# Two-layer cross-attention kernel on one core: queries' x loaded with features on partitions and normalised there, row statistics sent through DRAM; unit 0's row sums moved ahead

## The reference

```python
h = layernorm(x)                          # per row: (x - mean) / sqrt(var + 1e-5)
q = rope(h @ Wq)                          # 32 heads of 128
k = rope(ctx @ Wk); v = ctx @ Wv          # 8 heads of 128
logits = 30 * tanh(q @ k.T / sqrt(128) / 30)
w = softmax(where(mask, logits, -1e30))
x = x + (w @ v) @ Wo
```

## Time and profile before

| | |
|---|---|
| median of 3 runs | 824.38 us (824.3 to 824.47) |
| the profiled execution, its own time | 825.46 us |
| its span | 823.7 us |
| PE busy | 815.2 us (99%) |
| DVE, POOL, ACT busy | 591.5, 430.0, 403.7 us |
| mean granted TensorE clock | 0.996 |

### The profile page before, as it was taken

One profiled execution on the slowest core, in us unless ns is written; L12 is line 12 of the kernel. 1 busy time (PEld: TensorE's weight loads), 2 busy tenths in 40 slices (PEclk: granted clock), 3 DMA queues, 4 the chain that ended last, 5 costly groups with the idle time before them and its releaser, 6 DMA issues.

```text
span 823.7 us, 12087 instructions
## 1 busy us (share of the span) xinstructions
PE 815.2 (99%) x4310; PEld 674.5 (82%) x4310; DVE 591.5 (72%) x1133; ACT 403.7 (49%) x980; POOL 430.0 (52%) x341
## 2 busy tenths in 40 slices
PE   9999999899999999999999999999999999999998
PEld 7898877677777778777778788898988888888887
DVE  6874449889797988879788656464365667677894
ACT  6542114332334332343431532667797877777762
POOL 4665449874769667677864620113232531366442
PEclk9999999899999999999999999999999999999999
DMA  8545310413233223322311840002011200300002
GB/s 313 228 152 170 91 61 4 128 53 104 77 103 102 78 65 88 118 64 77 103 53 54 296 119 14 26 27 52 14 39 26 65 27 14 128 14 2 0 1 103
DMA packets 33244, 67.00 MB, mean 81 GB/s; under 512 B 5152, under 2 KB 8480, under 8 KB 32544
## 3 DMA queue, kind: packets, MB, share of 16 engines
q1 hardware_dynamic: 30640, 61.38, 24.0%
q10 hardware_dynamic: 2544, 4.85, 1.6%
HBM read 54.55 MB, written 11.67 MB: 80 GB/s over the span
## 4 chain that ended last, share of the span: by engine, by line
PE 73%; POOL 1%; issue 1%; DVE 0%; ACT 0%; DMA 0%; ACTq 0%; POOLq 0%
PE PB L1814 14%; PE PB L1816 13%; PE PB L1815 13%; PE PB L1862 11%; PE PB L2077 8%; PE PB L2092 3%; PE PB L1821 3%; PE PB L2004 3%; PE PB L1987 2%; PE PB L2025 1%; PE PB L2039 0%; POOL W L1200 0%; DMA stage<-in_wo 0%; POOL WVl L1200 0%; POOL WSl L1200 0%
## 5 line engine op out<-in xcount | busy, mean ns | idle before, releaser
L1237 POOL TENSOR_TENSOR qb<-qb,arena 128x512 f32<-128x512 f32 x76 | 99.6, 1316 | 126.2 <-DVE arena L1656 126.2
L1314 ACT ACTIVATE Oh<-PB 96x128 fp32r<-96x128 f32 (+2 forms) x236 | 79.3, 359 | 45.7 <-PE PB L2004 26.6
L1528 DVE TENSOR_TENSOR xs<-xs,PB 128x512 f32<-128x512 f32 x111 | 73.2, 682 | 36.8 <-PE PB L1816 27.9
L1200 POOL TENSOR_TENSOR WVl<-stage,WVh 128x512 fp32r<-128x512 f32 (+1 forms) x25 | 31.6, 1278 | 70.6 <-ACT WVh L1314 64.0
L1653 DVE TENSOR_TENSOR qb<-PB,ropeq 128x512 f32<-128x512 f32 x64 | 44.0, 688 | 26.6 <-PE PB L1816 16.1
L1814 PE MATMUL PB<-WVh,Oh 128*128 128x512 f32 x158 | 62.3, 394 | 0.8 <-DVE arena L1656 0.4
L1815 PE MATMUL PB<-WVl,Oh 128*128 128x512 f32 x158 | 61.5, 390 | 0.0
L1816 PE MATMUL PB<-WVh,Ol 128*128 128x512 f32 x158 | 61.5, 389 | 0.0
L1314 ACT ACTIVATE WSh<-wsum 128x1024 fp32r<-128x1024 f32 x12 | 12.7, 1061 | 90.8 <-POOL wsum L1182 90.8
L1814 PE MATMUL PB<-W,Oh 128*128 128x512 f32 x142 | 55.5, 391 | 0.6 <-POOL W L1200 0.6
L1815 PE MATMUL PB<-W,Oh 128*128 128x512 f32 x142 | 55.3, 389 | 0.0
(11 more groups left out here) (336 smaller groups left out, 2464.4 us busy)
## 6 DMA issues: line engine op xcount, KB each, us to landing
stage<-in_wq SPq DMA_DIRECT2D x44, 256.0 KB, 2.8
stage<-in_wo SPq DMA_DIRECT2D x44, 256.0 KB, 2.8
arena<-recs SPq DMA_DIRECT2D x32, 256.0 KB, 3.9
stage<-in_wk SPq DMA_DIRECT2D x12, 256.0 KB, 4.4
keys<-qb SPq DMA_DIRECT2D x12, 256.0 KB, 2.3
arena<-keys SPq DMA_DIRECT2D x6, 512.0 KB, 3.3
xs<-in_x SPq DMA_DIRECT2D x8, 256.0 KB, 6.6
ctx_hi<-cTh SPq DMA_DIRECT2D x1, 2048.0 KB, 7.4
```

The source lines that it names most:

```text
L1200: e.tensor_tensor(lo, src, hi.bitcast(f32), ALU.subtract).then_inc(s_wlo)
L1237: e.tensor_tensor(dst, dst, tmp, ALU.add).then_inc(s_radd)
L1314: return e.activation(dst, src, ACT.Copy)
L1528: e.tensor_tensor(xs[:, i, :], xs[:, i, :], PB[b][:, :], ALU.add).then_inc(free[b])
```

## The change

x is loaded a second time, transposed on the host (`xT`, 2 MB, four DMAs), into xf. DVE packs the reciprocal deviations and the negative mean times deviation of four tiles (two copies of 128x4), turns them with one transpose, and SyncE sends them as rows to DRAM (4 DMAs of 8 partitions) and reads them back broadcast to all partitions (2 DMAs), once for each half of the rows. DVE then normalises xf in place: for each half and each pair of feature chunks a multiplication and an addition of 128x1024 (`x_norm`, 8 instructions in all). ACT takes the high part and DVE the low part (`x_split`, 4 of 128x1024 on each). The 32 transposes on PE, the 8 `xn`, the 16 copies on ACT and the 8 `xsplit` on DVE go. In the plan the second four `stats` and `rstd` move ahead of three ropes, `v0(0, 3)` moves ahead of `k0(0, 1)`, `xt` moves behind `k0(5, 0)`, `ctx_out` (the store of the split ctx, 4 MB) moves there too, and the banks are dealt anew. In unit 0 `sum0` and its DMAs move ahead of `xt_split` and of two ropes; in unit 1 `norm0(0)` moves ahead of `q0p(1, 2)`, and `q0p(1, 2)` and `q0p(1, 3)` take banks 2 and 3.

```diff
     for i in LO:
         step("stats", 0, i)
     step("rstd", 0, 0)
+    step("xT_load")
+    step("stat_out", 0)
+    step("stat_in", 0)
...
-    for i in range(2):
-        stage("xT", 0, i)
-    ring[:] = [0, 1, 4, 6, 5, 2, 7]
+    ring[:] = [4, 5, 1, 6, 7, 0, 2]
+    stage("v0", 0, 3)
     stage("k0", 0, 1)
     step("rope", "k0", 1, 0)
...
+    for i in HI:
+        step("stats", 0, i)
+    step("rstd", 0, 4)
+    step("stat_out", 1)
+    step("stat_in", 1)
     step("rope", "k0", 0, 1)
+    k0(1, 1)
+    split("wk0", 3)
+    v0(0, 4)
+    k0(2, 0)
     stage("many")
     split("wv0", 1, 0)
     split("wv0", 1, 1)
...
     v0(0, 5)
-    for i in (4, 5):
-        step("xn", 0, i)
+    step("x_norm", 0, 0)
     k0(2, 1)
     spill_k(2, 0)
     split("wk0", 4)
     v0(0, 6)
     spill_k(2, 1)
...
+    step("x_norm", 1, 0)
     k0(3, 0)
+    for kk in range(2):
+        step("x_split", kk, 0)
     v0(0, 7)
...
     k0(3, 1)
+    step("x_norm", 0, 1)
     split("wk0", 5)
     v0(1, 0)
     spill_k(3, 1)
-    step("xt")
     v0(1, 1)
     k0(4, 0)
+    step("x_norm", 1, 1)
     split("wvq", 0)
...
     k0(4, 1)
+    for kk in range(2):
+        step("x_split", kk, 1)
     split("wk0", 6)
...
     k0(5, 0)
+    step("xt")
     split("wq0", 0)
     v0(1, 6)
+    step("ctx_out")
...
             burst(0)
             q0p(0, 1, 7)
             q0(1, 2, bank=1)
-            for k in range(2):
-                for h in range(2):
-                    step("xt_split", k, h)
+            step("sum0", 0)
+            step("sum0_out", 0)
+            for hf in range(2):
+                step("xt_split", 0, hf)
+            step("xt_split", 1, 0)
             q0p(0, 2, 0)
             q0p(0, 3, 4)
-            step("sum0", 0)
-            step("sum0_out", 0)
+            step("xt_split", 1, 1)
...
             q0p(1, 1, 1)
-            q0p(1, 2, 0)
+            norm0(0)
+            q0p(1, 2, 2)
             step("pair", 2)
-            norm0(0)
-            q0p(1, 3, 4)
+            q0p(1, 3, 3)
...
+                elif kind == "stat_out":
+                    hf, = k
+                    sp.wait_ge(s_turned, hf + 1)
+                    for b in range(4):
+                        e.dma_start(stat[:, 512 * hf:512 * hf + 512].rearrange("m (i b t) -> b m i t", b=4, t=32)[b],
+                                    pair[32 * b:32 * b + 8, 32 * hf:32 * hf + 32]).then_inc(s_sout, 16)
+                elif kind == "stat_in":
+                    hf, = k
+                    cols = slice(512 * hf, 512 * hf + 512)
+                    sp.wait_ge(s_sout, 64 * (hf + 1))
+                    for m in range(2):
+                        e.dma_start(stat_at[m][:, cols], stat[m, cols].unsqueeze(0).broadcast_to([128, 512])).then_inc(s_sin0[hf], 16)
...
+                elif kind == "x_norm":
+                    kk, hf = k
+                    x = xf[:, 2 * kk:2 * kk + 2, 512 * hf:512 * hf + 512]
+                    by, plus = (t[:, 512 * hf:512 * hf + 512].unsqueeze(1).broadcast_to([128, 2, 512]) for t in stat_at)
+                    for c in (2 * kk, 2 * kk + 1):
+                        dve.wait_ge(s_ldt[c], 16)
+                    dve.wait_ge(s_sin0[hf], 32)
+                    e.tensor_tensor(x, x, by, ALU.mult).then_inc(s_xm)
+                    dve.wait_ge(s_xm, 2 * hf + kk + 1)
+                    e.tensor_tensor(x, x, plus, ALU.add).then_inc(s_xf)
+                elif kind == "x_split":
+                    kk, hf = k
+                    lo, src, hi = (H[:, 2 * kk:2 * kk + 2, 512 * hf:512 * hf + 512] for H in (xTl, xf, xTh))
+                    dve.wait_ge(s_xhi, 2 * hf + kk + 1)
+                    e.tensor_tensor(lo, src, hi.bitcast(f32), ALU.subtract).then_inc(s_xlo)
```

More of the change, by code:

```diff
@@ L3 @@
 from contextlib import ExitStack
-INS = ["x", "ctxT", "tab", "lowtri", "wq0", "wk0", "wv0", "wvq", "wo0", "aw", "bcat",
+INS = ["x", "xT", "ctxT", "tab", "lowtri", "wq0", "wk0", "wv0", "wvq", "wo0", "aw", "bcat",
        "wq1", "wk1", "wv1", "wo1", "w1", "a1", "bf1", "coef", "scl", "bias"]
@@ L240, in plan @@
     split("wv0", 1, 1)
-    for i in HI:
-        step("stats", 0, i)
-    step("rstd", 0, 4)
-    k0(1, 1)
-    v0(0, 4)
-    step("ctx_out")
-    split("wk0", 3)
-    k0(2, 0)
     v0(0, 5)
-    for i in (4, 5):
-        step("xn", 0, i)
+    step("x_norm", 0, 0)
     k0(2, 1)
@@ L256, in plan @@
     spill_k(2, 1)
-    for i in (4, 5):
-        stage("xT", 0, i)
-        step("xn", 0, i + 2)
-        step("xsplit", 0, i)
+    step("x_norm", 1, 0)
     k0(3, 0)
+    for kk in range(2):
+        step("x_split", kk, 0)
     v0(0, 7)
@@ L264, in plan @@
     spill_k(3, 0)
-    for i in (6, 7):
-        stage("xT", 0, i)
-        step("xsplit", 0, i)
     k0(3, 1)
+    step("x_norm", 0, 1)
     split("wk0", 5)
@@ L829, in program @@
         wk0_1 = qb[:, 1, 0:512]
+        stat_at = [Eb[:, :, :].rearrange("p h c -> p (h c)"), rsum]
         small = []
@@ L1091, in sync_program @@
                     e.dma_start(xs[:, i, :], a["x"][i * 128:(i + 1) * 128, :]).then_inc(s_ldx[i], 16)
+                elif kind == "xT_load":
+                    for c in range(4):
+                        e.dma_start(xf[:, c, :], a["xT"][c * 128:(c + 1) * 128, :]).then_inc(s_ldt[c], 16)
+                elif kind == "stat_out":
[10 more added lines that the diff above has]
+                        e.dma_start(stat_at[m][:, cols], stat[m, cols].unsqueeze(0).broadcast_to([128, 512])).then_inc(s_sin0[hf], 16)
                 elif kind == "sum0_out":
@@ L1381, in scalar_program @@
                     move(xTh[:, :, 128 * i:128 * i + 128], src).then_inc(s_xhi)
-                    if ph == 0:
-                        move(xf[:, :, 128 * i:128 * i + 128], src).then_inc(s_xf)
+                elif kind == "x_split":
+                    kk, hf = k
+                    src, hi = (H[:, 2 * kk:2 * kk + 2, 512 * hf:512 * hf + 512] for H in (xf, xTh))
+                    act.wait_ge(s_xf, 2 * hf + kk + 1)
+                    move(hi, src).then_inc(s_xhi)
                 elif kind == "v0_move":
@@ L1396, in scalar_program @@
                     elif i < 2:
-                        act.wait_ge(*done("xT", 0, 7))
+                        act.wait_ge(s_xm, 4)
                     else:
@@ L1600, in vector_program @@
                     e.tensor_tensor(to[:, :], PB[bank_of("p", u, t)][:, :], kept, ALU.add).then_inc(s_cmb)
+                elif kind == "stat_out":
+                    hf, = k
+                    r = slice(4 * hf, 4 * hf + 4)
+                    dve.wait_ge(s_one, 2)
+                    dve.wait_ge(s_ln, 10 * (hf + 1))
+                    e.tensor_copy(psum32[:, 0:4], lnb[:, 1, r]).then_inc(s_stat)
+                    e.tensor_copy(psum32[:, 4:8], lnb[:, 4, r]).then_inc(s_stat)
+                    dve.wait_ge(s_stat, 2 * hf + 2)
+                    e.transpose(pair[:, 32 * hf:32 * hf + 32], psum32[:, :]).then_inc(s_turned)
+                elif kind == "x_norm":
[8 more added lines that the diff above has]
+                    e.tensor_tensor(x, x, plus, ALU.add).then_inc(s_xf)
+                elif kind == "x_split":
+                    kk, hf = k
+                    lo, src, hi = (H[:, 2 * kk:2 * kk + 2, 512 * hf:512 * hf + 512] for H in (xTl, xf, xTh))
+                    dve.wait_ge(s_xhi, 2 * hf + kk + 1)
+                    e.tensor_tensor(lo, src, hi.bitcast(f32), ALU.subtract).then_inc(s_xlo)
                 elif kind == "xt":
                     b = {(kk, hf): xf[:, 2 * kk:2 * kk + 2, 512 * hf:512 * hf + 512] for kk in range(2) for hf in range(2)}
-                    dve.wait_ge(s_xf, 8)
+                    dve.wait_ge(s_xlo, 4)
                     e.tensor_tensor(b[1, 0], b[1, 0], b[0, 0], ALU.subtract).then_inc(s_xt)
@@ L1834, in tensor_program @@
                     pe.wait_ge(*lo_ready("wp", u, t // 2))
-                    pe.wait_ge(*read("xT", 0, 4 * hf + 3))
+                    pe.wait_ge(*x_ready(hf))
                     for c in range(4):
@@ L1845, in tensor_program @@
                     pe.wait_ge(*(lo_ready("wp", u, t // 4) if t in (1, 2, 4) else (s_wslo, u - PLAIN + 1)))
-                    for i in (3, 7):
-                        pe.wait_ge(*read("xT", 0, i))
+                    pe.wait_ge(*x_ready(1))
                     if t in (4, 5, 6, 7):
@@ L1928, in tensor_program @@
                         pe.wait_ge(s_whi, splits["wq0", 0] + 1)
-                        pe.wait_ge(*read("xT", 0, 3))
+                        pe.wait_ge(*x_ready(0))
                         for c in range(4):
```

34 lines of the change are left out of this document (16 added, 18 removed).

## The result

The change takes 828.10 us (median of 6, 826.86 to 828.36) where the kernel before takes 824.28 (median of 6, 823.97 to 824.47): ratio 1.0045, 95% interval [1.0034, 1.0056]. It is slower by 3.8 us, inside the range, and 2.9 above the forecast of 825.2. The profiled execution took 828.36 us, span 826.6. In two of the nine executions of `combo`, further down, the clock was granted at 0.557 and 0.249 and they took 1351 and 3160 us; its ratio leaves them out, and so does the median given there.

The account below looks back on a forecast made before the run. PE was taken as the bound, busy 815 of 823.7 us. Terms -3.9 + 4.85 - 0.1 = +0.85 gave 826.3 us for a profiled execution, 825.2 as a median; range 818.5 to 829.5.

Parts of the forecast that it names:

- rival (a): First stage: PE's idle time before k0(7,0) drops the clock to 1.2 GHz, costing 3.2 us, giving 828.4; chance 0.22.
- PE's own work, -3.9: First stage: 32 transposes leave PE, 3.46 us plus 0.4 for switching, all of it on the path.
- The chain of DVE: First stage: DVE's instructions priced in order, x_norm(0,0) beginning at 31.75 and the rope of k0(5,1) ending at 76.2.
- rival (d): First stage: statistics arrive late behind xT, x_norm(0,0) starts 3 to 4 us late; 828 to 829, chance 0.10.
- Sum of waits, +4.85 forecast: First stage: PE waits for POOL's low parts, about 1.8 us at k0(6,0), 0.2 at k0(4,0), 2.85 at k0(7,0).
- The burst, -0.1: Burst of unit 2: norm0(0)'s wait goes, but POOL's additions and wo0 splits hold PE instead; net -0.1 us.
- the frame: Whole sum made against the profiled execution of 825.46 us, 1.08 above the median of 824.38.

Follow-up runs that it names:

- combo: The change with xt between k0(7,0) and k0(7,1), wk0 6 and 7 splits ahead of ropes, and unit 0's ropes ahead of DVE's two xt_split; 821.87 us, ratio 0.9970.
- before_burst: The kernel before with the change's orders and banks of units 0 and 1, unit 0's ropes ahead of DVE's xt_split, high parts first in e0(0,0); 823.87 us.
- ctx_out_back: The change with ctx_out, the store of 4 MB, back in its old place behind v0(0,4); 828.35 us, ratio 1.0049.
- low_last: The change with k0 from j = 2 on and v0(1,0) taking products with the weight's high part first, low part last; 825.83 us, ratio 1.0011.
- burst_only: The kernel before with only the change's new order and banks of units 0 and 1; 824.96 us, ratio 1.0000.
- filled: The change with ten extra matmuls of 512 columns issued where PE waits at k0(7,0), result unchanged; 827.35 us, ratio 1.0030.

## Why the prediction was right in range and 2.9 too low

The direction was right and the mechanism was the one at work, waits for POOL's low parts in the place of PE's work. The size was not: +0.9 forecast, +3.8 measured. The range was 11 us wide, and the median lies 0.3 from the number of rival (a), which was not the forecast.

- **PE's own work, -3.9: right** (3.8 in the page), and all of it went into a wait, as the forecast had it.
- **The chain of DVE, right in mechanism, 0.9 short.** It had the rope of `k0(5, 1)` end at 76.2; it ended at 77.1. `x_norm(0, 0)` began at 33.23, not 31.75. Of these 1.5 us 0.9 are one instruction that the working had priced as in the kernel before: the cast of `keep` took 0.19 there and 1.13 now, since the statistics' packing moved it beside a POOL instruction that starts at 15.11. Another 0.3 is the first `rstd`, which ended at 14.8 and not at 14.5. The pairs behind it cost what they were priced at or a little less (3.56 for the first, 3.6 forecast), which gave 0.6 back. `x_norm(0, 0)` followed `many` without a gap, so no statistics were late and rival (d) did not happen. `k0(7, 0)` came at 79.8, forecast 78.8.
- **Sum of waits, +4.85 forecast.** It stood for the distance between -3.9 and +0.95, and by that measure +5.9 were waits. The idle places are the named ones, `k0(6, 0)` 1.33 (1.8 forecast) and `k0(7, 0)` 2.44 (2.85), and two small ones, 0.50 at `v0(1, 0)` and 0.39 at `k0(4, 0)`. The number for `k0(6, 0)` is in part luck: the 21.6 us counted the second `x_split` pair, which stands behind the rope of `k0(4, 1)` and does not hold POOL. Without it that rope ends at 60.2 by the forecast's own prices (61.2 measured). The split was late all the same, done at 66.1, because POOL came from another split at 61.6 and needed 2.27 and 2.24 us for the addition and the split.
- **Rival (a), the clock: it happened, at half its price.** The forecast left it at 0.22. In this trace 1.5 us of the 3.5 are the half clock behind `k0(7, 0)`; the rival had said 3.2, read off the burst, where the stretch at 1.2 GHz was twice as long. Its argument against itself, that waits of 0.7 us left the clock alone, does not carry: in `before_burst` the clock fell behind waits of 0.73. The Trainium skill, page "TensorE: Matmul & The Clock Gate", section "HAM oscillation — how this bites in real kernels", has it that a group of matmuls behind a wait for data starts at the low clock, told of a kernel with waits of 3 to 5 us. The trace agrees at 2.44 us of idle time. It isn't so in each execution: `ctx_out_back` had 2.47 and a clock of 1.000 in its profile, `low_last` 2.02 and 1.000, with 0.998 in 5 of 12 timed executions.
- **The burst, -0.1: right in its waits.** `d0(0)` no longer waits, `b0(2)` idles 1.79 for POOL's additions, and the last wo0 split ends at 165.9, which less the shift of 3.5 is 162.4 (forecast 163.05). Against the profiled execution it gave back 0.73. Against the median `burst_only` measures 0.0, within 0.09% either way, and at equal clock it costs 0.95.
- **The step that was furthest off is the frame.** The sum was made against the profiled execution, 1.08 over the median, and the 1.08 was taken off again at the end, as if the changed kernel had it too. But it was the half clock in the burst of this one execution, which the change takes away; its own profile is 0.26 over its median. So 0.8 of the 2.9 are here, 1.5 are the clock at `k0(7, 0)`, 0.9 the DVE chain, and the burst gave back 0.6 more than forecast; what remains, 0.3, is less than the scatter between executions.

The executions under 2 bear this step out: without the 1.08 taken off, -0.1 for the burst is +0.98 against a kernel whose clock doesn't fall, and `burst_only` at 1.000 is 0.95 slower than such a kernel. There is a second sum, in executions at 1.000 alone. `k0(7, 0)` starts 1.66 later, measured from `k0(1, 0)`, or 1.97 as the traces stand, and the new order of the burst costs 0.95: together 2.6 to 2.9. `filled`, whose clock never falls, is 2.8 above the kernel before at 1.000 in its group (827.35 and 824.51 on average). That leaves about 1 of the 3.8 us of the medians for the clock; `filled` itself took back 0.75. The chances add up to 0.32, 0.27 and 0.41 for faster, same and slower; the forecast had written 0.28 and 0.40.

## What to carry to other kernels

Before moving work from a bound engine to one that is full for tens of us, write down when the full engine delivers what the bound one needs next. If that time is fixed by the full engine, the saving turns into idle time there, and waits that one finds along the way don't add up (6.0 expected, 2.3 got). The cure was not less work but another place in a queue: a split ahead of an addition that waits for another engine, or 8 us of work with a late due time moved to where its engine has slack, took back 3.3 and 4.2 us where the change had cost 3.8. And look at the granted clock of the profiled execution before making a sum against it, and compare two kernels in executions of the same clock: a reorder that measured 0.0 in the medians cost 0.95 that way.
